# Fill multiplications of the unit matrix in front of eight waits of TensorE, in a two-layer decoder kernel

## The reference

```
x    : (4, 512, 512)
L0 a : layer norm, in_proj (512 -> 2320), SSD in chunks of 64, gate silu(z), out_proj, + x
L0 b : rms-like norm, softmax attention over a context (4, 512, 512) with a mask, + x
L0 c : router picks 128 of 512 tokens of each sequence (weights, threshold, positions),
       these are gathered, pass 512 -> 2048 -> 512 with gelu, and are scattered back, + x
L1 a : attention of 16 heads over the 4 sequences at each position, qkv and proj, + x
L1 b : fp8 quantised activations times a quantised context (512 -> 512), + x
L1 c : ternary feed-forward 512 -> 1408 -> 512, silu gate, int8 activations, + x
```

## Time and profile before

| | |
|---|---|
| median of 3 runs | 1134.84 us (1134.48 to 1134.9) |
| profiled execution | 1137.32 us |
| its span, first to last instruction | 1135.6 us |
| mean granted TensorE clock | 0.968 |
| TensorE busy | 1033.6 us, 91% |
| VectorE, ScalarE, GpSimd busy | 74%, 56%, 42% |

### The profile page before, as it was taken

How to read it: one execution, slowest core, us unless ns; L and a number is a source line. 1 busy time by engine, 2 the same in 40 slices (tenths; PEclk the granted TensorE clock), 3 DMA queues, 4 the chain that set the end, 5 groups by cost and what they waited for, 6 DMA issues and landing times.

```text
span 1135.6 us, 14829 instructions
## 1 busy us (share of the span) xinstructions
PE 1033.6 (91%) x4894; PEld 757.2 (67%) x4894; DVE 844.6 (74%) x1607; ACT 641.2 (56%) x1241; POOL 474.0 (42%) x727
## 2 busy tenths in 40 slices
PE   5889999999999999869899869997888999999896
PEld 4667888788878888646566557775655666666442
DVE  5777766776677676726988748858888978979873
ACT  4644444344434443226566547574468889888773
POOL 5343324332433233314888513205553554634420
PEclk9799999999999999889999979999999999999898
DMA  8200000000000000143210016420001112111122
GB/s 294 97 1 1 1 1 1 1 1 1 1 1 1 2 1 1 38 171 160 77 38 1 1 57 231 141 110 0 1 5 23 40 32 49 31 41 36 36 65 74
DMA packets 48428, 52.94 MB, mean 47 GB/s; under 512 B 34528, under 2 KB 35552, under 8 KB 46048
## 3 DMA queue, kind: packets, MB, share of 16 engines
q1 hardware_dynamic: 48352, 51.99, 14.4%
HBM read 39.92 MB, written 4.19 MB: 39 GB/s over the span
## 4 chain that ended last, share of the span: by engine, by line
PE 59%; DVE 18%; POOL 8%; ACT 7%; issue 6%; DMA 1%; DVEq 0%; POOLq 0%; ACTq 0%
PE bank L410 47%; PE bank L495 4%; PE bank L418 3%; DVE cum_h L910 1%; PE bank L486 1%; PE bank L506 1%; DVE prod L1376 1%; DVE half_lo L1260 1%; PE bank L476 1%; DVE spare L1169 1%; DVE y L946 1%; PE bank L728 1%; ACT eT L1927 1%; DVE at L1388 1%; POOL a_rs L2081 1%
## 5 line engine op out<-in xcount | busy, mean ns | idle before, releaser
L410 PE MATMUL bank<-win_hi,a_uT_hi 128*128 128x512 f32 (+1 forms) x320 | 129.6, 405 | 5.0 <-DVE a_uT_lo L854 3.1
L410 PE MATMUL bank<-win_lo,a_uT_hi 128*128 128x512 f32 (+1 forms) x320 | 122.4, 383 | 0.0
L410 PE MATMUL bank<-win_hi,a_uT_lo 128*128 128x512 f32 (+1 forms) x320 | 121.9, 381 | 0.0
L1617 ACT ACTIVATE ex<-bank 128x48 f32<-128x48 f32 x16 | 3.4, 210 | 148.2 <-PE bank L454 148.2
L2175 POOL TENSOR_TENSOR y<-y,off 128x512 f32<-128x512 f32 x24 | 37.7, 1572 | 114.9 <-DVE off L931 114.9
L410 PEld LDWEIGHTS bank<-win_hi,a_uT_hi 128*128 128x128 f32 x320 | 62.4, 195 | 19.9 <-issue 6.4
L410 PEld LDWEIGHTS bank<-win_lo,a_uT_hi 128*128 128x128 f32 x320 | 62.4, 195 | 12.9 <-issue 2.6
L410 PEld LDWEIGHTS bank<-win_hi,a_uT_lo 128*128 128x128 f32 x320 | 62.1, 194 | 11.7
L495 PEld LDWEIGHTS bank<-xs,wgt 128*128 128x128 f32 x512 | 62.6, 196 | 9.2 <-issue 6.6
L410 PE MATMUL bank<-wq,eT 128*128 128x512 f32 x128 | 61.8, 628 | 6.6 <-ACT eT L1927 6.5
L410 PE MATMUL bank<-f,fqT_next 128*128 128x512 fp8e4 (+1 forms) x312 | 64.1, 362 | 1.4 <-DVE x L1501 1.4
(11 more groups left out here) (342 smaller groups left out, 3149.5 us busy)
## 6 DMA issues: line engine op xcount, KB each, us to landing
wchunk<-w_in SPq DMA_DIRECT2D x32, 256.0 KB, 4.2
stage<-f_in SPq DMA_DIRECT2D x4, 1408.0 KB, 6.1
x<-x_in SPq DMA_DIRECT2D x16, 256.0 KB, 6.0
land<-win_in SPq DMA_DIRECT2D x4, 1024.0 KB, 8.5
wq<-ctxT_in SPq DMA_DIRECT2D x4, 1024.0 KB, 8.5
ctx<-ctx_in SPq DMA_DIRECT2D x4, 1024.0 KB, 5.9
out<-x SPq DMA_DIRECT2D x16, 256.0 KB, 2.0
first_stage<-f_in SPq DMA_DIRECT2D x2, 1408.0 KB, 14.1
```

Of the source, the lines that this page charges most:

```text
L410: made = e.matmul(bank, a, b, start=start and n == 0, stop=stop and n == len(pairs) - 1)
```

## The change

A helper `keep_busy(bank, count)` multiplies the unit matrix with itself `count` times into the first 128 columns of a bank. Each product begins the bank anew (`start=True`), and the step that has claimed the bank overwrites them later. It is called in eight places, each after the claim of the bank and in front of the wait for the operands. Nothing else differs.

```
+            def keep_busy(bank, count):
+
+                for _ in range(count):
+                    e.matmul(bank[:, 0:P], ident[:], ident[:], start=True, stop=True)
 turn_un(i)
                 w.wait_ge("consts", 2)
+                if i == 0:
+                    keep_busy(bank, 14)
                 w.wait_ge("u_ready", i + 1)
 project(i, n)
+                if i == 0 and n == 0:
+                    keep_busy(bank, 9)
                 w.wait_ge("win_lo", n + 1)
                 w.wait_ge("uT_lo", i + 1)
 spread_weights
+                if b == BATCH - 1:
+                    keep_busy(bank, 15)
                 w.wait_ge("weighed", b + 1)
 positions
+                if b == BATCH - 1:
+                    keep_busy(bank, 15)
                 w.wait_ge("route_step", 7 * b + 5)
 gather
+                if b == BATCH - 1:
+                    keep_busy(bank, 4)
                 w.wait_ge("picked", b + 1)
 turn_du
+                if n == 0:
+                    keep_busy(bank, 6)
                 w.wait_ge("u_ready", 2 * NT + n + 1)
 turn_eu
+                if n == NT - 3:
+                    keep_busy(bank, 5)
                 w.wait_ge("eu_ready", n + 1)
 f_down
+                if n == NT - 1:
+                    keep_busy(bank, 15)
                 w.wait_ge("hq_turned", 16 * n + 16)
```

## The result

The changed kernel takes 1126.95 us in the median of 4 runs (1125.62 to 1127.69), against 1134.87 us before (4 runs, 1134.48 to 1136.55). The ratio is 0.9923, with a 95% interval of 0.9907 to 0.9939: by the medians 7.9 us faster, as forecast (1126.9); by the ratio 8.7 us, within 6.9 to 10.6. The profiled execution took 1126.93 us, with a span of 1125.2 us and a mean granted clock of 0.983, against 1137.32, 1135.6 and 0.968 before.

What follows compares the result with a forecast made beforehand. TensorE, 59% of the chain, was taken to bound the kernel where others wait for its slow-clock work. Gains 0 + 2.58 + 1.60 + 2.15 + 2.26 = 8.6 us, less 0.7, gave 7.9 us: 1126.9 us, range 1123.7 to 1131.5.

Steps and rivals of the forecast that it cites:

- The price of a fill: One unit-matrix product on TensorE: 0.234 us, as in the gather, with bounds of 0.16 and 0.47 us.
- Places 1 and 2: The kernel's start, up to the first projections: 0 us gained, with -0.5 to +0.1, since VectorE sets the pace.
- Places 3 to 5: The last sequence's routing: transposes 0.49, `positions` 0.41 and last gather 1.68 us quicker, 2.58 us in all.
- Place 6: The scatter in front of `qkv_product`: 3.48 us shortens to 1.88, so 1.60 us gained.
- Place 7: `e_product` in front of `attend_out`: shortens by 3.03 us, of which 2.15 us count because ScalarE's copy waits behind `f_h`.
- Place 8: The last `f_down`: 4.80 us shortens to 2.54, and all 2.26 us count.
- The allowance of 0.7 us: Taken off the gain for unfilled waits from the feed-forward on, where one more clock fall is likelier than one less.
- Some falls stay or move: Rival: clock falls in one or two fill remainders or two more unfilled waits, losing 2 to 5 us; chance 0.17.
- The front gains are taken back: Rival: the second layer's VectorE and GpSimd work binds, places 3 to 6 give nothing, 4.4 us left, 1130.4; chance 0.07.
- The fills don't hold the clock: Rival: unit-matrix products don't keep the clock up at the waits, all stays as before, 1134.8 us; chance 0.04.
- slower: Rival: fills run at 1.2 GHz, 0.47 us each, and overhang their waits, 8.0 us more, 1142.8 us; chance 0.04.
- The signs: Clock 1.00 at places 3 to 8; wrong if fills exceed 0.31 us, remainders lose clock, or new 0.50 stretches appear 670-1120 us.

Runs made afterwards that it cites:

- 6 alone: The kernel before with fills at place 6 only, the scatter in front of `qkv_product`: 1134.93 us, ratio to before 0.9999.
- 1 and 2 alone: The kernel before with fills only at places 1 and 2, at the start: 1134.49 us, ratio to before 0.9998.
- 7 and 8 alone: The kernel before with fills only at places 7 and 8, `e_product` and the last `f_down`: 1130.44 us, ratio to before 0.9961.
- the moved `wproj_lo` without fills: The kernel before with only GpSimd's `wproj_lo` subtraction moved ahead of the second tile's mean and deviation: 1135.62 us, ratio to before 1.0005.
- six fills: The changed kernel with 6 fills instead of 15 at places 3, 4 and 8: 1131.5 us, ratio to before 0.9974.
- The four groups alone: The kernel before with fills only at places 3 to 5, 6, 1 and 2, or 7 and 8: ratios to before 0.9965, 0.9999, 0.9998, 0.9961.

## Why the prediction was right

**The price of a fill** was right: 3.51 us for 15, 0.234 us for each, the gather's price; at 1.2 GHz 0.51 us for each, against my 0.47. At place 1 the clock rose only during the fills, and the 14 took 5.82 us (0.42 us each), within the bound that I had set.

**Places 1 and 2** were right at 0: the two alone have a ratio of 0.9998.

**Places 3 to 5** were predicted at 2.58 us and gave 2.61 in the trace. Of the 4.0 us that they gave alone (2.6 to 5.4), the rest has a place: the feed-forward from its first product to the first scatter takes 95.64 us in the changed kernel (666.67 to 762.31) and 97.22 us before (670.86 to 768.08), though nothing in it was changed. The wait of 1.75 us in its middle is there in both, but in the changed kernel the clock stays up behind it. The changed kernel's stretches (length, busy of TensorE, its weight loads, VectorE, ScalarE and GpSimd, clock, DMA):

```profile
724.00:728.00 4.00, 4.00 (x19) 3.23 (x18) 3.94 (x6) 2.71 (x5) 0.00 (x0) 1.00 0.67 206
812.50:815.00 2.50, 2.50 (x7) 1.45 (x6) 2.36 (x6) 1.69 (x4) 2.02 (x3) 0.50 0.00 0
```

In the profiles of all six kernels whose last gather was slow (before, 6 alone, 1 and 2 alone, 7 and 8 alone, the moved `wproj_lo` without fills, six fills) the clock fell behind this wait; in the eight whose gather was fast it did not. Why the one decides the other was not tried, but it is a term of +1.6 us that I had only as a chance.

**Place 6** is the step that failed. I wrote that `qkv_product` stands behind the scatter, that "VectorE and ScalarE wait for that product", and took 1.60 us. The scatter did shorten by that, and the product did come earlier. What I didn't look at is what VectorE's next instruction would run beside: GpSimd's `wproj_lo`, which doesn't move with TensorE. `prod` took 3.08 us instead of 1.41 and ended when it had ended before. The term measured 0: alone 0.9999, and 10.86 against 10.90 us in the trace. With GpSimd's instruction moved, 1.05 us of it came back locally. Nor did I see that the idle 2.14 us would have a fall of its own.

**Place 7** was predicted at 2.15 us of 3.03, for ScalarE's `f_h` in front of its copy: 2.17 us. **Place 8**: 2.26 predicted, 2.25 in the trace. Together alone, 4.4 predicted and 4.4 measured. The four groups alone add up to 4.0 + 0 + 0 + 4.4 = 8.4 us.

**The allowance of 0.7 us** for stretches that move had the right subject and missed the size on both sides. The wait in the feed-forward gave +1.6 us, and in the second layer one stretch more fell than before: behind a wait of 1.69 us, at 812.5 to 815 us above. (The fall at 781 us stands in place of the one under the scatter, and costs nothing.) From the first to the last transposes of `d_u` it is 252.48 us before, 252.51, 252.52 and 252.49 us in the three single-place kernels without places 3 to 5, and 253.13 us in the changed kernel, 0.65 us more.

The changed kernel's trace then adds up to 2.61 + 1.58 + 0 - 0.6 + 2.3 + 2.25 = 8.1 us (2.3 being 60.91 - 58.62, from place 7's transposes to the last `f_down`). Measured were 7.9 us by the medians, 8.7 by the ratio. The place that gave nothing and the fall that vanished unasked offset each other: the number was right in part by luck. The 10.4 us between the two spans are no measure of the change, as 1.6 us of them lie ahead of place 3, where profiles of the same program differ by up to 2.9 us, and 0.7 us lie behind the last addition: from its start to the end of the span it is 3.9 us in this profile of before, and 3.2 us in each of the other thirteen profiles.

**The rivals.** "Some falls stay or move" was true of the unfilled waits, not of the filled ones: rests of 0.4 to 1.5 us didn't lower the clock at any of the places 3 to 8. "The front gains are taken back" was true of place 6 alone. "The fills don't hold the clock" and "slower" fell, the latter shown in small with six fills.

**The signs.** By one of its own signs the prediction was wrong: new stretches at 0.50 do stand behind waits between 670 and 1120 us, at 781 and 812 us. The fills of place 1, at the low clock, also last 0.42 us each, over its 0.31. One reading in the rivals was wrong too. I took the 0.42 us between the three runs before as a sign that stretches don't come and go in this kernel. But its profiled execution lay 2.48 us over their median, and 21 later runs of the kernel before, timed together, spread from 1133.53 to 1137.1 us.

On transposes, the Trainium skill (TensorE: Matmul & The Clock Gate, Part 4: PE-mode transpose) says that the full clock doesn't engage for them, as they don't count as work in the same way. These runs differ: four transposes take 0.65 us, 28 of them at the start raise the clock, and 30 of them in a wait keep the gather behind them at 3.84 us. On the number of slow products the Trainium skill (TensorE: Matmul & The Clock Gate, Part 1) says that it varies between runs of one kernel. The changed kernel's two profiles agree with that: in the mixer's end the clock is low from 467 to 475 us in the one and from 470 to 474 in the other, and in the second layer from 812 to 816 in the one and from 828 to 832 in the other.

## What to carry to other kernels

Work without use in front of a long wait is worth what the slow work behind the wait costs, where that work is in the chain, and only as far as the next engine can take it up; follow each saved microsecond to the instruction that consumes it, and look at what that one then runs beside on another engine. Size the fill so that little of the wait stays empty, and so that it still ends in time at the high clock: rests of up to 1.5 us kept the clock up at all of the places 3 to 8, 2.01 and 3.4 us lost it, 5.75 us of fill overran. That is no limit for waits in general, since the clock also fell behind unfilled waits of 1.22 and 1.56 us. After a fill the fall can stand behind a later wait (as at place 6 and at the mixer's end), so price a fill by the whole stretch up to a fixed mark, not by the step behind it.

## What was not expected of the hardware

VectorE's 128x512 float32 product took 0.69 us alone, and 3.08 us beside a GpSimd subtraction of 128x2048 (4.57 us), ending only half a microsecond behind it. With an overlap of 0.86 us it took 1.41 us, and again ended half a microsecond behind.

Whether the clock falls behind a wait of 1.5 to 2.1 us differs from place to place in one execution, and repeats between kernels. Behind the attention's wait of 1.56 us in front of `ctx_hi,pT_hi`, near 562 us, it fell in all fourteen profiles; behind the second layer's wait of 2.06 us in front of `wproj_hi,oT_hi`, near 877 us, in none. So the length of a wait alone does not decide. And behind the feed-forward's wait of 1.75 us it fell in six of six profiles with a slow last gather, and in none of eight with a fast one. What links them stays open.
